# Two-layer kernel: layer two's down-step low-rank product in float32 over four column groups, and a search with sums of 4 values

## The reference, cut to what matters

```
def _lora_linear(x, W, A, B, adapter_indices):
    base = jnp.einsum('bsd,df->bsf', x, W)
    lora = jnp.einsum('bsr,brf->bsf', jnp.einsum('bsd,bdr->bsr', x, A[adapter_indices]), B[adapter_indices])
    return base + lora
gate = _lora_linear(x, Wg, Ag, Bg, adapter_indices)
up = _lora_linear(x, Wu, Au, Bu, adapter_indices)
h = jax.nn.silu(gate) * up
return _lora_linear(h, Wd, Ad, Bd, adapter_indices)
...
sel_p, sel_idx = jax.lax.top_k(score, capacity)   # layer one, for each expert
```

## Time and profile before

| | us |
|---|---|
| median of 3 runs (619.18 to 620.15) | 619.51 |
| the profiled execution | 619.69 |
| its span, first to last instruction | 617.9 |
| PE busy in the span | 579.7 |
| DVE busy | 357.5 |
| ACT busy | 249.3 |

### The profile page before, as it was taken

One profiled execution on the slowest core, in us unless ns is written; L12 is line 12 of the kernel. 1 busy time (PEld: TensorE's weight loads), 2 busy tenths in 40 slices (PEclk: granted clock), 3 DMA queues, 4 the chain that ended last, 5 costly groups with the idle time before them and its releaser, 6 DMA issues.

```text
span 617.9 us, 9782 instructions
## 1 busy us (share of the span) xinstructions
PE 579.7 (94%) x3366; PEld 483.5 (78%) x3366; DVE 357.5 (58%) x794; ACT 249.3 (40%) x550; POOL 130.1 (21%) x111
## 2 busy tenths in 40 slices
PE   4765799999999999999999999999999999999994
PEld 2533589999999999968888888888888888888883
DVE  6888865875785666645454454454464544544533
ACT  2643246756865755663422322333134223223110
POOL 3000224452462461662002020030030120000000
PEclk9986999999999999999999999999999999999998
DMA  8998667353347340731004023031040040210012
GB/s 309 337 299 266 201 238 241 43 153 80 36 136 258 36 68 6 218 61 44 1 1 136 10 83 63 1 124 23 0 130 15 8 130 7 83 29 2 14 22 34
DMA packets 63932, 60.90 MB, mean 99 GB/s; under 512 B 37328, under 2 KB 56272, under 8 KB 62544
## 3 DMA queue, kind: packets, MB, share of 16 engines
q1 hardware_dynamic: 52880, 37.99, 20.6%
q0 software_dynamic: 8832, 22.09, 14.5%
q10 hardware_dynamic: 2176, 0.26, 0.3%
HBM read 45.05 MB, written 19.47 MB: 104 GB/s over the span
## 4 chain that ended last, share of the span: by engine, by line
PE 87%; DVE 7%; DMA 2%; ACT 2%; issue 1%; SPq 1%; DVEq 0%
PE bank L1193 24%; PE bank L1195 23%; PE bank L1194 23%; PE bank L1438 5%; PE bank L1405 2%; PE bank L1403 2%; DMA xT<-in_xT 2%; DVE passed L846 2%; PE bank L1265 1%; PE bank L1397 1%; PE bank L1301 1%; PE bank L1292 1%; PE bank L1412 1%; PE bank L1413 1%; PE bank L1461 1%
## 5 line engine op out<-in xcount | busy, mean ns | idle before, releaser
L689 ACT ACTIVATE act<-bank 128x512 f32<-128x512 f32 x64 | 38.3, 599 | 186.3 <-PE bank L1438 186.3
L1150 DVE TENSOR_TENSOR prod<-bank,act 128x512 f32<-128x512 f32 x64 | 44.2, 691 | 110.2 <-PE bank L1438 109.0
L1052 DVE TENSOR_TENSOR hid_lo<-hf,hid_hi 128x512 fp32r<-128x512 f32 (+1 forms) x72 | 45.5, 633 | 51.2 <-ACT hf L625 50.9
L1193 PE MATMUL bank<-w_hi,hid_hi 128*128 128x256 f32 x256 | 71.7, 280 | 0.0
L1195 PE MATMUL bank<-w_hi,hid_lo 128*128 128x256 f32 x256 | 71.4, 279 | 0.0
L1194 PE MATMUL bank<-w_lo,hid_hi 128*128 128x256 f32 x256 | 71.4, 279 | 0.0
L622 ACT ACTIVATE hid_hi<-bank 128x512 fp32r<-128x512 f32 (+1 forms) x72 | 39.8, 552 | 64.9 <-PE bank L1195 64.8
L450 POOL DMA_INDIRECT xg<-flat_rows,slot_row x32 | 34.2, 1069 | 127.5 <-DVE slot_row L912 80.0
L461 POOL DMA_INDIRECT x_rows<-y_sb,slot_row x32 | 51.8, 1617 | 43.0 <-ACT y_sb L590 32.5
L1193 PE MATMUL bank<-xs_hi,w_hi 128*128 128x512 f32 (+1 forms) x148 | 55.2, 373 | 1.8 <-DVE xs_lo L922 1.3
L480 POOL DMA_INDIRECT b_pair<-b_rows,b_row x8 | 8.7, 1085 | 222.0 <-PE bank L1461 221.4
(11 more groups left out here) (278 smaller groups left out, 1269.6 us busy)
## 6 DMA issues: line engine op xcount, KB each, us to landing
w_raw<-in_L_ffn_W SPq DMA_DIRECT2D x8, 1024.0 KB, 6.9
flat_rows<-x_sb SPq DMA_DIRECT2D x8, 520.0 KB, 10.6
xT<-in_xT SPq DMA_DIRECT2D x8, 512.0 KB, 9.2
x_sb<-in_x SPq DMA_DIRECT2D x8, 512.0 KB, 8.3
outT<-out_sb SPq DMA_DIRECT2D x120, 32.0 KB, 1.6
b_rows<-b_all_hi SPq DMA_DIRECT2D x1, 1152.0 KB, 9.8
b_rows<-b_all_lo SPq DMA_DIRECT2D x1, 1152.0 KB, 12.2
wdT<-in_wdT SPq DMA_DIRECT2D x1, 1024.0 KB, 5.9
```

The source lines that it names most:

```text
L689: act.activation(act1[h % 2][:, :], bank[h % 2][:, :], ACT.Silu).then_inc(silu1, 1)
L1052: dve.tensor_tensor(lo[:, n], hf[s % 2][:, n], hi[:, n].bitcast(f32), ALU.subtract).then_inc(hid0, 1)
L1150: dve.tensor_tensor(prod[h % 2][:, :], bank[2 + h % 2][:, :], act1[h % 2][:, :], ALU.mult).then_inc(prod1, 1)
L1193: pe.matmul(out, lh, rh, start=start, stop=False, skip_group_check=True)
```

## The change

Layer two: `with_pair` and its 16 matmuls a tile go. In their place `low_rank_down` issues 8 float32 matmuls a tile with weights of 32 columns, in one block: the product of hidden chunk h goes to column group h mod 4, and so into partitions 32 (h mod 4) and on of bank 6. It stands in step 1 of the next tile ahead of the last `down1_`, and for the last tile in two parts ahead of its last two `down1_`. Its operands are `prod` (the float32 hidden chunk, now kept for all 8 steps) and `ad_pair` (A columns, not split). The four partial sums are added by `finish`, which multiplies by B rows that stand four times under each other, now with both halves: 6 matmuls a tile where there were 2. These rows have a DRAM tensor of their own, `bd_rows`, and two indirect DMAs a tile; `b_rows` gets shorter by them. The A matrices of the down step are no longer split in layer one (two operations less on ACT and on DVE).

Search: a count is 8 matmuls of 112 columns (28 by 4 sums), the 16 later row products stand behind steps 0 to 9 as 2, 2, 2, 2, 2, 2, 1, 1, 1, 1, and `wfT_s` is made in step 8.

```diff
-ROWB = 2 * HID + D
+ROWB = 2 * HID
+SUMS = 4
+        a_pair = [sb(f"a_pair{i}", [P, KD, 4, 32], f32r) for i in range(2)]
+        ad_pair = [sb(f"ad_pair{i}", [P, KH, 32], f32) for i in range(2)]
+        bd_pair = [sb(f"bd_pair{i}", [P, 2, D], f32r) for i in range(2)]
...
-        ROWS_FIRST, FOLD_STEP = 16, 8
+        ROWS_FIRST, WF_STEP = 16, 8
+        ROW_STEPS = [2, 2, 2, 2, 2, 2, 1, 1, 1, 1]
...
+            def gather_bd(t):
+                if t >= 2:
+                    pool.wait_ge(acc1, t - 1)
+                for i in range(2):
+                    pool.indirect_dma_start(
+                        out=bd_pair[t % 2][:, i, :].bitcast(f32), out_offset=None, in_=bd_rows[:, :],
+                        in_offset=bass.IndirectOffsetOnAxis(ap=bd_row[:, i, t:t + 1], axis=0)).then_inc(bd_in[t % 2], 16)
...
             gather_x1(1)
+            for t in range(2):
+                gather_bd(t)
             for t in range(2, NB1):
                 gather_x1(t)
                 gather_b(t)
+                gather_bd(t)
...
-                dve.scalar_tensor_tensor(vs[:, :], vm_hi[:, :].bitcast(f32), cols[:, 6:7], vm[:, :], ALU.mult, ALU.add
-                                         ).then_inc(v_lo, 1)
+                dve.tensor_tensor(vs[:, :], vm[:, :], vm_hi[:, :].bitcast(f32), ALU.subtract).then_inc(v_lo, 1)
...
-                    for t in range(2):
-                        g = slice((2 * half + t) * 8, (2 * half + t + 1) * 8)
-                        last = pe.matmul(bank[7][:, 0:E * CAND * 8], ones_b[:, :],
+                    for t in range(G // 2 // SUMS):
+                        g = slice(half * G // 2 + t * SUMS, half * G // 2 + (t + 1) * SUMS)
+                        last = pe.matmul(bank[7][:, 0:E * CAND * SUMS], ones_b[:, :],
...
-            def with_pair(out, par, i, rhs, start, stop):
-
-                hi, lo = rhs
-                pe.matmul(out[:, :], a_pair[par][:, i, :, :].rearrange("p a r -> p (a r)"), hi, start=start, stop=False,
-                          skip_group_check=True)
-                return pe.matmul(out[0:96, :], a_pair[par][:, i, 0:3, :].rearrange("p a r -> p (a r)"), lo, start=False, stop=stop,
-                                 skip_group_check=True)
+            def low_rank_down(t, par, steps):
+
+                pe.wait_ge(prod1, KH * t + steps[-1] + 1)
+                for h in steps:
+                    r = slice(32 * (h % 4), 32 * (h % 4) + 32)
+                    last = pe.matmul(bank[6][r, :], ad_pair[par][:, h, :], prod[par][h][:, :], start=h < 4, stop=h >= 4,
+                                     skip_group_check=True, tile_position=(0, 32 * (h % 4)))
+                if steps[-1] == KH - 1:
+                    last.then_inc(v_mm, 1)
...
-            def finish(t, par, halves=False):
+            def finish(t, par, pair, halves=False):
 
                 pe.wait_ge(v_lo, t + 1)
+                pe.wait_ge(bd_in[par], 32 * (pair + 1))
                 for k in range(KD):
-                    last = pe.matmul(bank[4 + k][:, :], b_pair[par][:, 2 * HID + k * P:2 * HID + (k + 1) * P], vs[:, :],
-                                     start=False, stop=True, skip_group_check=True)
+                    bd_hi, bd_lo = (bd_pair[par][:, i, k * P:(k + 1) * P] for i in range(2))
+                    pe.matmul(bank[4 + k][:, :], bd_hi, vm_hi[:, :], start=False, stop=False, skip_group_check=True)
+                    pe.matmul(bank[4 + k][:, :], bd_lo, vm_hi[:, :], start=False, stop=False, skip_group_check=True)
+                    last = pe.matmul(bank[4 + k][:, :], bd_hi, vs[:, :], start=False, stop=True, skip_group_check=True)
...
                     pair_half(par, pair, 1, uu[par], bank[2 + h % 2], h, up1, t)
+                    if h == 1 and not first:
+                        low_rank_down(t - 1, 1 - par, range(KH))
...
+            for i in range(2):
+                low_rank_down(NB1 - 1, 1, range(4 * i, 4 * i + 4))
             down1_(KH * NB1 - 2, KH - 2, NB1 - 1, 1, False, ends=True)
```

More of the change, by code:

```diff
@@ L252, in adaln_moe_lora @@
         act1 = [sb(f"act1_{i}", [P, BT], f32) for i in range(2)]
-        prod = [sb(f"prod{i}", [P, BT], f32) for i in range(2)]
+        prod = [[sb(f"prod{j}_{i}", [P, BT], f32) for i in range(2)] for j in range(2)]
+        prod_rest = [sb(f"prod{i}", [P, BT], f32) for i in range(2, KH)]
+        prod = [p + prod_rest for p in prod]
         out_sb = [sb(f"out_sb{i}", [P, KD, BT], f32) for i in range(2)]
@@ L302, in adaln_moe_lora @@
                                                     sem("ids_in"))
-        b_in = [sem(f"b_in{i}") for i in range(2)]
+        b_in, bd_in = ([sem(f"{n}{i}") for i in range(2)] for n in ("b_in", "bd_in"))
         a_in = sem("a_in")
@@ L1262, in _ @@
                     pe.wait_ge(asked, 2 * i + half + 1)
-                    for t in range(2):
-                        g = slice((2 * half + t) * 8, (2 * half + t + 1) * 8)
-                        last = pe.matmul(bank[7][:, 0:E * CAND * 8], ones_b[:, :],
+                    for t in range(G // 2 // SUMS):
+                        g = slice(half * G // 2 + t * SUMS, half * G // 2 + (t + 1) * SUMS)
+                        last = pe.matmul(bank[7][:, 0:E * CAND * SUMS], ones_b[:, :],
                                          passed[:, :, :, g].rearrange("p e j g -> p (e j) g"),
-                                         start=half == 0 and t == 0, stop=half == 1 and t == 1, skip_group_check=True)
+                                         start=half == 0 and t == 0, stop=half == 1 and t == G // 2 // SUMS - 1,
+                                         skip_group_check=True)
                 last.then_inc(counted, 1)
-                if i < FOLD_STEP:
-                    for n in range(G - 2 * FOLD_STEP + 2 * i, G - 2 * FOLD_STEP + 2 * i + 2):
-                        item(n)
+                for n in range(ROWS_FIRST + sum(ROW_STEPS[:i]), ROWS_FIRST + sum(ROW_STEPS[:i + 1])):
+                    item(n)
             pe.wait_ge(ranks_in, 1)
@@ L1446, in down1_ @@
                     pe.wait_ge(prod1, s + 2)
-                last = with_pair(bank[6], par, KD + h, at(hid1[h % 4], every, every), h == 0, h == KH - 1)
-                if h == KH - 1:
-                    last.then_inc(v_mm, 1)
                 for k in range(KD):
@@ L1475, in steps1 @@
                     if h == 2 and not first:
-                        finish(t - 1, 1 - par)
+                        finish(t - 1, 1 - par, pair if par else pair - 1)
                     if not (first and h < 2):
@@ L1524, in _ @@
             steps1(NB1 - 1, 1, NB1 // 2 - 1, False, True)
+            for i in range(2):
+                low_rank_down(NB1 - 1, 1, range(4 * i, 4 * i + 4))
             down1_(KH * NB1 - 2, KH - 2, NB1 - 1, 1, False, ends=True)
             down1_(KH * NB1 - 1, KH - 1, NB1 - 1, 1, False, ends=True)
-            finish(NB1 - 1, 1, halves=True)
+            finish(NB1 - 1, 1, NB1 // 2 - 1, halves=True)
 def kernel(**inputs):
```

42 lines of the change are left out of this document (21 added, 21 removed).

## The result

The kernel takes 613.92 us after the change (median of 4 runs, 613.2 to 614.18), beside 619.83 us for the kernel before (4 runs, 619.18 to 620.39): a ratio of 0.9903, 95% interval 0.9886 to 0.992. The profiled execution took 613.93 us, of which its span is 612.1. The forecast was 611.2. Two executions of this case, one of `e4_loads_behind_gather` (3,214.51 us) and one of `f1_after_again` (1,997.02 us), took several times as long as the others of the same kernels, for a cause that no run here shows, and are left out of every time here.

A forecast was written before the change was run, and what follows sets the result against it. PE was taken to bound layer two, a DVE-PE chain the search. Layer two -7.6 and start -0.8 (search -1.6, 0.8 given back) sum to -8.4: from 619.6 to 611.2 us, range 609.0 to 615.0.

The forecast's parts named there:

- -0.77 us: Layer two, net per tile: -3.68 for the pairs that go, +0.91 for `finish`, +2.0 for the float32 block.
- 2.0 us: Layer two's float32 block per tile: 1.73 for four rounds, 0.05 issue, 0.2 for group changes; bounds 1.73 and 2.6.
- -7.6: Layer two in all: -7.7 us up to the last `pair_half`, and +0.1 from there to `out_sb`.
- +0.1: End of the program: `out_sb` starts at 610.25 instead of 610.11, since the first bank needs three matmuls.
- 0.12 us less in each of 10 steps: Search: the reduction on DVE falls from 224 to 112 elements at 1.05 ns an element, -1.2 us.
- 1.6: Search in all: 1.6 us less, from -2.1 to -0.9, by the shorter reduction and moving `wfT_s`, less +0.15 for counts.
- 0: Search steps 8 and 9: PE's clock may hold or not with one row product behind steps 6 to 9, counted as 0.
- I take the middle, 4.3 us ... 0.8 us given back: Start: first gather lands between 2.9 us in quiet and 5.8 beside loads, giving back 0.8 us of the search's gain.
- rival 2: Start gives back all and more, through late rows or folds at half clock; +0.8 to +3, 612 to 614.2; 12%.
- -0.8: Start: the search's gain of 1.6 us less 0.8 us given back by the later gather; from -2.0 to +1.0.
- three signs that the prediction named for being wrong: Block starts in pairs or single records; gather landing over 6 us after issue; half PE clock during folds behind the routing.
- PE without gaps: Between the search and layer two's end: PE has no gaps, so the start's gain or loss goes through to the end.

The follow-up runs named there:

- e4_loads_behind_gather: The changed kernel with all seven of layer two's weight loads held until the first tile's gather has landed; 612.21 us, ratio 0.9872.
- f1_after_again: The whole changed kernel run again without alteration, as the reference on one chip; median 614.54 us, ratio 0.9899 to the kernel before.
- e3: The changed kernel with the row products behind steps 0 to 7 again, two each, all else as changed; 611.8 us, ratio 0.9873.

## Why the prediction came out as it did

**Layer two: right.** "-0.77 us" a tile was -0.79; the block's "2.0 us" was 2.05, near the low bound and far from 2.6; from tile 0's first gate matmul to `out_sb` (278.39 to 610.11 before, 280.37 to 604.41 after) it is 324.04 us where it was 331.72, so -7.7 for the forecast's -7.6. The rows that gave it were those of the same form, `z_products`, and the argument that its overlap doesn't depend on length. The Trainium skill, "TensorE: Matmul & The Clock Gate", section "Measured speedup vs the span model", states 3.07 times for four row groups and 2.38 times for three column groups, from which the prediction estimated 2.45 us. This case's traces, with four column groups in float32, don't agree with that estimate: 7.05 us in one group against 1.92 in four is 3.7 times. The end of the program got 0.24 us longer, for +0.1.

**The search: nearly right.** The reduction measures 272 ns where "0.12 us less in each of 10 steps" gives 269. In all it brought 1.34 us for the forecast's 1.6, and 1.34 to 1.79 in the seven traces with row products up to step 9; in the three with row products by step 7 it brings 1.9 to 2.1. So row products in steps 8 and 9, taken as "0", cost some 0.4 us on average. Part of it is the clock: in the trace after, the last two steps' counts take 1.09 us at half clock and a step there 2.79 us, where e3 keeps its step of 2.65; the parts were not tried apart.

**The start: wrong, and this is the step that failed.** "I take the middle, 4.3 us ... 0.8 us given back." The gather was issued 10.43 us behind A as before, but landed after 6.2 us, more than the 5.8 that was the high bound, since it met loads issued at 59.30 that ran to about 72.3. That gives back 2.83 us. Choosing the middle between a quiet gather and one beside other loads had no row for it: the gather's issue lay wholly inside the loads' time, so the high end was the nearest row. The loads also began later than thought: 4.17 us later behind S, not 3.2 (3.5 to 4.2 in the traces with late loads). The second half is the clock, +2.07, which the sum had at nothing and rival 2 described. With both, S to Q became 3.55 us longer where "-0.8" was forecast, outside the stated -2.0 to +1.0.

Two of the three signs that the prediction named for being wrong came: the gather landed over 6 us after its issue (6.24), and PE's clock was half while the folds ran (0.68 on average from 64 to 67). The folds at half clock (5.41 us for 3.72) were hidden by the wait for the rows, though; what cost was the clock behind that wait. The sentence that all between the search and layer two is "PE without gaps" doesn't hold either for the first tile: there PE has gaps before and after, and the clock falls there.

**Luck in the number.** Rival 2's price, "+0.8 to +3" for 612 to 614.2, looks right beside 613.92, but is not: against the forecast the start was 4.35 us worse. The number is where it is because S came 1.5 us sooner, which no term of the prediction has. With the S of before it would have been about 615.4, outside the range of 609.0 to 615.0.

On how a gather shares with loads the trace allows one thing more. The gather landed at 71.76, and the last load, issued at 62.42 and so 3.1 us ahead of it, landed 11.3 us later, at 73.7. So the gather did not wait for the loads to finish, but took 6.24 us beside them where it takes 2.9 in quiet. The Trainium skill, "DMA: Bandwidth & Descriptors", section "Queues, rings and completion order", has each engine go round between the queues that have work; the trace agrees with that in so far as the gather overtook the last load.

**How the miss adds up.** Start +3.55 for -0.8 is +4.35; layer two -0.1; and -1.5 us from `xT` landing sooner, ahead of anything that the prediction costed: +2.75 against 613.92 - 611.2 = 2.7. S lay between 28.08 and 30.73 in thirteen traces. The two with the old layer two have the latest (29.68 and 30.73; all others 29.48 or less), so that part of this 1.5 us belongs to the change is not excluded; layer two alone measures 8.7 and 9.2 us where its rows give 7.7. That stays open.

## What to carry to other kernels

Small matmuls with few weight columns were worth four column groups here: what counted was rounds of four, not their order. A gain in a stage that ends in a transfer is only as good as what the transfer then meets: moving the last store two steps later moved 3.75 MB of loads on top of gathers of 128 rows each and cost more than the stage had saved. Ask of every moved store what is queued behind it on its engine, and price a gather that is issued inside a bulk load at the full length of the collision, with the pause that this makes for PE. And check a forecast by its stages: here the total fell into the range while one stage lay outside its own.

## What the runs showed of the hardware

- In one column group 16 float32 records of 512 columns start 0.43 us apart; in four groups, four at a time every 0.43 us, in either order of groups. Records last 592 ns (median) in all three.
- Changing from the full array to column groups and back costs about 0.3 us in all at the most: 2.05 us for four rounds of 0.433.
- The same kernel had the clock at 1.00 in one execution and at 0.50 for some 3.4 us in another, at the same place behind a pause of PE, worth up to 1.6 us; 8 matmuls of filler ahead of the pause and 3 more inside it went with a clock of 1.00 (one trace).
- A gather of 128 rows took 2.9 to 3.0 us in quiet, 4.0 where loads were nearly over, and 5.9 to 6.2 inside 3.75 MB of loads on another queue.
